# Causal attention on one core: four key tiles share one denominator matmul

## The reference

```python
x = x + _L0_attn_ref(_layernorm(x, axis=-1), wq, wk, wv, wo)     # causal attention, 32 query heads, 8 key heads of 32
x = x + _L0_ffn_ref(_layernorm(x, axis=-1), ...)                 # a mixing layer
x = x + _L1_attn_ref(_layernorm(x, axis=-1), Wq, Wk, Wv, Wo)     # causal attention again
x = x + _L1_ffn_ref(_layernorm(x, axis=-1), ...)                 # experts
```

```python
scores = einsum('bqhd,bkhd->bhqk', q, k) / sqrt(32)   # masked above the diagonal
attn = softmax(scores, axis=-1)
out = einsum('bhqk,bkhd->bqhd', attn, v)
```

## Time and profile before

| | us |
|---|---|
| time of the program, median of 3 executions | 3196.64 (3193.96 to 3196.96) |
| span of the profiled execution, first to last instruction | 3192.5 |
| TensorE matmul busy in the span | 2861.6 (90%) |
| VectorE busy | 2039.7 (64%) |
| ScalarE busy | 1004.8 (31%) |
| GpSimd busy | 282.5 (9%) |
| 3072 matmuls of the denominators, busy together | 329.9 |

### The profile page before, as it was taken

One profiled execution on the slowest core, in us unless ns is written; L12 is line 12 of the kernel. 1 busy time (PEld: TensorE's weight loads), 2 busy tenths in 40 slices (PEclk: granted clock), 3 DMA queues, 4 the chain that ended last, 5 costly groups with the idle time before them and its releaser, 6 DMA issues. The chain is left out here.

```text
span 3192.5 us, 48849 instructions
## 1 busy us (share of the span) xinstructions
PE 2861.6 (90%) x16848; PEld 1854.1 (58%) x16848; DVE 2039.7 (64%) x3303; ACT 1004.8 (31%) x1549; POOL 282.5 (9%) x397
## 2 busy tenths in 40 slices
PE   7999998999999799752869999989999997897999
PEld 6555454655554488642656555546555553786887
DVE  7676677767776433588776766767677774324443
ACT  2234334224334411252521433433234334201000
POOL 1011011001110000000010001011011110001111
PEclk9999999999999899875979999999999999998999
DMA  4322222323121322000133213213313120544111
GB/s 154 91 62 86 62 61 80 111 63 101 54 81 51 124 84 75 0 0 0 79 132 116 75 53 87 69 55 103 104 53 100 53 80 20 193 138 152 67 63 43
DMA packets 121063, 253.16 MB, mean 79 GB/s; under 512 B 12720, under 2 KB 39728, under 8 KB 120880
## 3 DMA queue, kind: packets, MB, share of 16 engines
q1 hardware_dynamic: 120912, 251.03, 24.8%
HBM read 166.57 MB, written 84.41 MB: 79 GB/s over the span
## 5 line engine op out<-in xcount | busy, mean ns | idle before, releaser
L597 DVE TENSOR_REDUCE a_mx<-a_psh 128x1 f32<-128x512 f32 (+3 forms) x1216 | 773.2, 660 | 351.5 <-PE a_psh L743 236.8
L502 ACT ACTIVATE a_prob<-a_pst 128x1024 f32<-128x1024 f32 (+3 forms) x768 | 595.9, 816 | 823.3 <-PE a_pst L789 821.0
L738 PE MATMUL a_psh<-a_kst,a_qst 96*128 96x512 f32 (+3 forms) x1536 | 543.6, 404 | 9.4 <-DVE a_mx L597 3.4
L738 PEld LDWEIGHTS a_psh<-a_kst,a_qst 96*128 96x128 f32 x1536 | 287.4, 192 | 396.8 <-DVE a_mx L597 327.4
L789 PE MATMUL a_pst<-a_qst,a_kst 97*128 97x512 f32 (+2 forms) x1536 | 424.3, 377 | 46.6 <-issue 17.5
L809 PE MATMUL a_ppv<-a_prob,a_vg 128*32 128x512 f32 (+3 forms) x3072 | 333.7, 507 | 12.5 <-POOL a_prob L436 11.1
L789 PEld LDWEIGHTS a_pst<-a_qst,a_kst 97*128 97x128 f32 x1536 | 256.6, 196 | 138.6 <-issue 72.3
L809 PE MATMUL a_pden<-a_prob,a_ones 128*32 128x512 f32 (+3 forms) x3072 | 329.9, 502 | 0.0
L436 POOL TENSOR_SCALAR_AFFINE_SELECT a_prob<-a_prob 128x512 f32<-128x512 f32 x256 | 178.6, 698 | 1383.7 <-ACT a_prob L502 1383.7
L641 DVE RECIPROCAL a_dens<-a_dens 128x512 f32<-128x512 f32 x64 | 214.6, 3353 | 68.2 <-ACT a_dens L510 55.2
L743 PE MATMUL a_psh<-a_negmask,a_identb 128*128 128x128 bf16 x1024 | 228.7, 232 | 0.0
(11 more groups left out here) (213 smaller groups left out, 3786.8 us busy)
## 6 DMA issues: line engine op xcount, KB each, us to landing
a_qst<-q SPq DMA_DIRECT2D x192, 256.0 KB, 4.5
a_wraw<-in_wqkv SPq DMA_DIRECT2D x52, 512.0 KB, 5.6
q<-a_stg_hi SPq DMA_DIRECT2D x64, 256.0 KB, 2.5
q<-a_stg_lo SPq DMA_DIRECT2D x64, 256.0 KB, 2.8
oT<-a_oT SPq DMA_DIRECT2D x64, 256.0 KB, 2.5
a_kst<-kT SPq DMA_DIRECT2D x96, 128.0 KB, 3.0
h_oraw<-oT SPq DMA_DIRECT2D x16, 512.0 KB, 4.1
h_x<-in_x SPq DMA_DIRECT2D x16, 512.0 KB, 4.7
```

Source lines behind the costliest of these rows:

```text
L502: act.activation(prob[k % 2][:, 2 * half:2 * half + 2, off:], pst[:, half, :, off:], ACT.Exp, scale=scale).then_inc(s["exp_done"], 1)
L597: dve.tensor_reduce(mx_hq[kc][:, heads[0]:heads[0] + m, qt], psh[:, at, 0:m * n].rearrange("p (m n) -> p m n", n=n), AX.X, ALU.max)\
L738: mm = pe.matmul(psh[:, at, i * n:(i + 1) * n], qst[par][0:96, h, qt * P:(qt + 1) * P], kst[par][0:96, kc * BANK:kc * BANK + n], start=Tru ...
```

## The change

Units 4 to 7 are called held. It holds for all orders but `ahead7`, so for 30 groups.

- ScalarE writes the exponentials of unit 4 into `acc`, which is `xin0` (heads 0, 1) and `xin1` (heads 2, 3), and not into `prob`.
- The four denominator steps den 4 to den 7 are gone. PV 4 reads `acc`.
- For units 5, 6 and 7 GpSimd adds the first half of `prob` to `acc[0]` and VectorE the second half to `acc[1]`, each one instruction of 128 x 1024 elements. GpSimd's comes where ST k.1 stands in the list, VectorE's where den k stood.
- At den 9, behind that unit's own 4 matmuls, 4 matmuls over `acc` bring the sum into the denominators. They wait for both chains of additions.
- ScalarE's exponentials of units 7, 8 and 9 wait, beside what they waited for, for GpSimd's addition of unit 5, 6 and 7 (first half) and VectorE's (second half), since these read the `prob` that is overwritten.
- SyncE waits in `ahead7` for the last PV of the group before, ahead of its first load into `xin0`.
- The `_turn` semaphores are counted up beside the waits and nobody waits for them.

```diff
@@ -45,6 +45,9 @@
 UNITS = [(qc, ki) for qc in range(NQC) for ki in range(4 * qc + 4)]
 NU = len(UNITS)
 DIAGONAL = [e for e, (qc, ki) in enumerate(UNITS) if ki >= 4 * qc]
+FIRST_FULL = UNITS.index((1, 0))
+ADDED = [e for e, (qc, ki) in enumerate(UNITS) if qc == 1 and 1 <= ki <= 3]
+SUMMED_AT = UNITS.index((1, 5))
 CHUNK_END = [e for e, (qc, ki) in enumerate(UNITS) if ki == 4 * qc + 3]
 
 
@@ -200,7 +203,7 @@
         "wl0", "wl1", "w_hi", "w_ready", "sh_ready", "sh_free", "roped", "q_hi", "q_lo", "v_ready",
         "k_out", "q_out", "qs00", "qs01", "qs10", "qs11", "ks0", "ks1", "mx_ready", "mT_ready", "m_out", "mr0", "mr1", "st_ready",
         "exp_done", "mask_done", "pv_done", "acc_copied", "norm_done", "vg_ready", "os0", "os1",
-        "pool_turn", "sp_turn", "pe_turn")}
+        "pool_added", "dve_added", "pool_turn", "act_turn", "dve_turn", "sp_turn", "pe_turn")}
     x_first, x_loaded = [s[f"xf{i}"] for i in range(NX_BUF)], [s[f"xl{i}"] for i in range(NX_AHEAD)]
     w_loaded = (s["wl0"], s["wl1"])
     max_row, o_stored = (s["mr0"], s["mr1"]), (s["os0"], s["os1"])
@@ -261,6 +264,7 @@
                                          for p in prob for i in range(2)]
 
 
+        acc = [x[:, :].rearrange("p (h n) -> p h n", n=BANK) for x in xin]
         x_next = [x[:, :] for x in xin] + [vT[:, :], wraw[0][:, :, :].rearrange("p k n -> p (k n)")]
         mx_hq = [mx[:, i, :].rearrange("p (h q) -> p h q", q=ST_) for i in range(2)]
         block = ctx.enter_context(nc.Block())
@@ -276,6 +280,12 @@
         def psh_banks(k, half):
 
             return psh[:, half, :]
+
+        def exps(order, e, half):
+
+            if order is not ahead7 and e == FIRST_FULL:
+                return acc[half]
+            return prob[e % 2][:, 2 * half:2 * half + 2, :]
 
         def batches(eng, batch):
 
@@ -363,6 +373,8 @@
 
                             sp.wait_ge(s["w_ready"], W0 + (b + 1) * N_WCHUNK + 1)
                             sp.sem_inc(s["sp_turn"], 1)
+                            sp.wait_ge(s["pv_done"], PV0 + n * NU)
+                            sp.sem_inc(s["sp_turn"], 1)
                         if k >= NX_AHEAD:
 
                             sp.wait_ge(s["zT_ready"], ZT0 + ((b + 1) * ST_ + k - NX_AHEAD) * 2 + 2)
@@ -436,6 +448,17 @@
                         pool.affine_select(out=blk, in_=blk, compare_op=ALU.is_ge, fill=0.0, base=0,
                                            pattern=[[0, GH], [1, P]], channel_multiplier=-1)\
                             .then_inc(s["mask_done"], 1)
+                    if what == "ST" and half == [1] and e in ADDED and order is not ahead7:
+
+                        pool.wait_ge(s["exp_done"], E0 + (n * NU + e) * 2 + 2)
+                        if e == ADDED[0]:
+                            pool.sem_inc(s["pool_turn"], 1)
+                            pool.wait_ge(s["pv_done"], PV0 + n * NU + FIRST_FULL + 1)
+                        else:
+                            pool.sem_inc(s["pool_turn"], 1)
+                            pool.wait_ge(s["pool_added"], (b * (NG - 1) + g) * len(ADDED) + ADDED.index(e))
+                        pool.sem_inc(s["pool_turn"], 1)
+                        pool.tensor_tensor(acc[0], acc[0], exps(order, e, 0), ALU.add).then_inc(s["pool_added"], 1)
                     if what == "XS":
                         reciprocal_deviation((b + 1) * ST_ + e, e)
                 if order is body:
@@ -498,8 +521,13 @@
                         if half == 0:
 
                             act.wait_ge(s["pv_done"], n * NU + k + 1)
+                        if k - 2 in ADDED and order is not ahead7:
+
+                            adds = (b * (NG - 1) + g) * len(ADDED) + ADDED.index(k - 2) + 1
+                            act.wait_ge((s["pool_added"], s["dve_added"])[half], adds)
+                            act.sem_inc(s["act_turn"], 1)
                         act.wait_ge(s["st_ready"], ST0 + (n * NU + k) * 2 + half + 1)
-                        act.activation(prob[k % 2][:, 2 * half:2 * half + 2, off:], pst[:, half, :, off:],
+                        act.activation(exps(order, k, half)[:, :, off:], pst[:, half, :, off:],
                                        ACT.Exp, scale=scale).then_inc(s["exp_done"], 1)
                     if what == "PV" and part == [1] and k in CHUNK_END:
                         q = n * 2 + CHUNK_END.index(k)
@@ -630,6 +658,16 @@
                         normalise((b + 1) * ST_ + k, x_next[k % NX_AHEAD], k)
                     if what == "XC":
                         xT_lo((b + 1) * ST_ + k, k, psh_banks)
+                    if what == "PV" and step[2] == 1 and k in ADDED and order is not ahead7:
+
+                        if k == ADDED[0]:
+                            dve.wait_ge(s["pv_done"], PV0 + n * NU + FIRST_FULL + 1)
+                        else:
+                            dve.wait_ge(s["dve_added"], (b * (NG - 1) + g) * len(ADDED) + ADDED.index(k))
+                        dve.sem_inc(s["dve_turn"], 1)
+                        dve.wait_ge(s["exp_done"], E0 + (n * NU + k) * 2 + 2)
+                        dve.sem_inc(s["dve_turn"], 1)
+                        dve.tensor_tensor(acc[1], acc[1], exps(order, k, 1), ALU.add).then_inc(s["dve_added"], 1)
                     if what == "LO":
                         part_lo(b * RB + 4 + (g + 2 - k) * 2 + k, k)
                     if what == "WS":
@@ -804,11 +842,28 @@
                             if ki == 0:
 
                                 pe.wait_ge(s["acc_copied"], (n * 2 + qc) * 2 + 2)
-                        acc, lhs = ((ppv, vg[par][:, ki, :]), (pden, ones[:, :]))[part]
-                        for h in range(GH):
-                            mm = pe.matmul(acc[h * HD:(h + 1) * HD, off:], lhs, prob[k % 2][:, h, off:],
-                                           start=(ki == 0), stop=(ki == 4 * qc + 3), skip_group_check=True)
-                        if part == 1:
+                        if part == 0:
+                            for h in range(GH):
+                                mm = pe.matmul(ppv[h * HD:(h + 1) * HD, off:], vg[par][:, ki, :],
+                                               exps(order, k, h // 2)[:, h % 2, off:],
+                                               start=(ki == 0), stop=(ki == 4 * qc + 3), skip_group_check=True)
+                        held = order is not ahead7 and k in (FIRST_FULL, *ADDED)
+                        first_den = (ki == 4 if order is not ahead7 and qc == 1 else ki == 0)
+                        if part == 1 and not held:
+                            for h in range(GH):
+                                mm = pe.matmul(pden[h * HD:(h + 1) * HD, off:], ones[:, :], prob[k % 2][:, h, off:],
+                                               start=first_den, stop=(ki == 4 * qc + 3), skip_group_check=True)
+                        if part == 1 and k == SUMMED_AT and order is not ahead7:
+
+                            adds = (b * (NG - 1) + g + 1) * len(ADDED)
+                            pe.wait_ge(s["pool_added"], adds)
+                            pe.sem_inc(s["pe_turn"], 1)
+                            pe.wait_ge(s["dve_added"], adds)
+                            pe.sem_inc(s["pe_turn"], 1)
+                            for h in range(GH):
+                                mm = pe.matmul(pden[h * HD:(h + 1) * HD, :], ones[:, :], acc[h // 2][:, h % 2, :],
+                                               start=False, stop=False, skip_group_check=True)
+                        if part == (0 if held else 1):
                             mm.then_inc(s["pv_done"], 1)
 
             pe.wait_ge(s["const"], 1)
```

## The result

The changed kernel takes 3381.59 us (median of four executions, 3341.5 to 3408.5) against 3196.66 (3193.96 to 3196.96) before. The kernel is slower, as forecast, but by 177 us where 73 were forecast, and outside the range given. The profiled execution took 3374.12 us, with a span of 3372.4; TensorE's mean granted clock was 0.891 in it, and 0.947 before.

What follows compares the result with a forecast made beforehand. TensorE was taken to lead, with VectorE close behind through two banks. Terms -0.4 + 1.15 + 0.7 + 0.25 + 1.0 = +2.7 us in 28 groups, +75.6 on 3196.6, gave 3272, rounded to 3270; range 3228 to 3308.

Steps and rivals of the forecast that it cites:

- the chain of each unit: PV, S steps, their maxima, VectorE's addition, one more maximum, then the S step needing that bank; +2.7 us per group.
- unit 4: Den step gone and no addition: S12 comes earlier, the stalled start goes, PV 5 about 0.4 us earlier; term -0.4.
- unit 5: VectorE's addition waits for GpSimd's, ends at PV 5 +4.1; S19 starts at +4.85, before 3.70; term +1.15 us.
- unit 6: VectorE's addition, behind GpSimd's, ends at PV 6 +4.35; S25 starts at +5.1, before 4.42; term +0.7 us.
- unit 7: No GpSimd addition beside VectorE's, which ends at +3.77; S30 starts at +4.4, before 4.15; term +0.25 us.
- the sum at unit 9: Four matmuls over `acc` at den 9, neither waiting nor hidden: +1.0 us per group.
- Three of the prediction's signs: `pden` busy time falls about 90 us; S matmuls wait 60 us or more for maxima; VectorE's unit 5 addition about 1.9 us.
- the later addition waits for the earlier: When VectorE's and GpSimd's additions meet, the later waits for the earlier's end; unit 5's ends at +2.9 + 1.2 = +4.1.
- The other reading, both slowed all along: Both engines slowed while additions overlap, VectorE to about 0.37 of its pace; sum 0.1 us smaller per group.
- rival 4: Additions collide more or TensorE's clock falls: a group loses 3.9 us or more, 3306 us and beyond; chance 0.14.
- `body7`: The two groups without S steps: TensorE's saving held back by GpSimd's additions; bounds -1 and +2 us per group, taken at 0.
- The cover named for GpSimd's additions: One 2.4 us addition per about 5 us unit costs nothing; without cover, unit 8's mask and PV 8 would be late.

Runs made afterwards that it cites:

- Experiment 2: Changed kernel with all additions and waits kept, but TensorE makes all denominators as before and the matmuls over the sum are left out: 3268.94 us, ratio 1.0234.
- experiment 1: Changed kernel without the additions on both engines and their waits, so the denominators lack units 5 to 7: 3131.57 us, ratio 0.9804.
- experiment 5: Changed kernel with VectorE's addition one place earlier in its queue, at PV k's first part, GpSimd not made to wait: 3163.34 us, ratio 0.9906.
- experiment 3: Changed kernel with GpSimd's additions for units 6 and 7 waiting until VectorE's for the unit before is done: 3283.02 us, ratio 1.0278.
- experiment 6c: Changed kernel with VectorE's addition one place earlier and S steps spread again by TensorE's real columns, GpSimd not made to wait: 3154.75 us, ratio 0.9882.

## Why the prediction was wrong

**Right: what bounds, and the chain of each unit.** VectorE's queue behind the two banks of S was the path. By the steps of the prediction, in the group that kept its clock: unit 4 -0.40 (said -0.4); unit 5 +1.37 (+1.15), with S19 at PV 5 + 5.08 (+4.85); unit 6 +0.75 (+0.7), with S25 at PV 6 + 5.07 (+5.1); unit 7 +0.17 (+0.25), its addition 1.22 alone; the sum at unit 9 +0.87 (+1.0). Together 2.76, forecast 2.7. Experiment 2 shows the same waits, and experiment 1 the same path without additions. The unit 5 difference is small and is where GpSimd started: 0.97 after PV 5 (516.90), not 0.5. Three of the prediction's signs came as well: the matmuls into `pden`, the sum's included, are busy 236.4 us where they were 329.9, 93.5 less (said 90), the S matmuls wait 102.9 us for maxima (said 60 or more), and VectorE's addition for unit 5 is stretched, to 2.30 (said 1.9).

**Right: the later addition waits for the earlier.** 2.30 where 1.22 is the time alone, an end 1.1 after GpSimd's, and in experiment 5 the reverse. The Trainium skill, "SBUF — State Buffer", section "Who interferes with whom", calls the shared pair of ports an exclusive lock and says that the order of issue decides who blocks; that it is held for the whole instruction it says where it speaks of VectorE's two-port modes. These rows agree with a lock for the whole instruction, in both directions. The other reading, both slowed all along, falls: the engine that began first was not slowed in the changed kernel (2.36). In experiment 5 VectorE's was not either (1.22).

**The step that failed: the clock, for which the sum has no term.** The prediction left "the clock falls" to rival 4, which shares its chance of 0.14 with a worse collision. The new idle ahead of S19 was foreseen, at about 1.5 us (it is 1.85), and was said to lie near the two stretches of the earlier trace rows, busy 1.90 of 3 us at a clock of 1.00 and 1.45 at 0.54. But the rest of the stretch was not added up. With den 5 gone there are only S17, S18 and half of ST 7 between S16 and S19, and TensorE's busy time is well below both:

```profile
397.40:400.40 3.00, 0.97 (x3) 0.49 (x3) 3.00 (x4) 1.02 (x1) 1.30 (x1) 0.97 0.00 0
```

The clock then fell in 26 of 28 groups and stayed down for 3 to 20 us, mostly 10 or 20, in which the matmuls take nearly twice as long: 122 us in all. The prediction's own sign for rival 4, a granted clock under 0.95 in the stage, came: 0.89 from the first group to the last of layer 0, before 0.98. Rival 4 had the right cause, but its price began at 1.2 us per group over the forecast (3306, "and beyond"); measured are 4.4. Experiments 2 and 5 show it by its absence: with more work on TensorE between the waits, or with the waits shortened, the mean clock is 0.942 and 0.948, and the time 105 and 211 us less than the changed kernel's.

**Mis-sized: `body7`.** Taken at 0 with bounds -1 and +2, measured +3.1 and +3.3. The cover named for GpSimd's additions was lost, by the path that the prediction named for it: the three run back to back, the mask of unit 8 is late behind them, and PV 8 waits.

```profile
1158.60 1.93 PE L847 MATMUL a_ppv<-a_prob,a_vg 128*32 128x512 f32 x8 [2.03 <-POOL a_prob L448]
```

```profile
1150.55 3.13 POOL L461 TENSOR_TENSOR a_xin<-a_xin,a_prob 128x1024 f32<-128x1024 f32 x1 [0.18 <-POOL a_xin L461]
```

The PV at 1158.60 again runs at the low clock (1.93). GpSimd's additions also take more here (3.13), beside VectorE's, which the estimate of 7.1 us left out; VectorE's take up to 3.2.

**Not seen: the four waits at group starts**, 29 us in the trace of before, which the shorter program lost. That hid part of the loss: had they stayed, the result would have been about 3403.

**Open.** In the group of the rows at 515.93 the same wait (1.82 us) with the same little work (0.97 of the 3 us from 518.00 on) left the clock at 1.00; in most groups it fell. What decides this was not tried. That the kernel's times spread over 67 us, where the kernel before spreads over 3, fits a clock that falls in some groups of one execution and not of another (the four executions had mean clocks of 0.891, 0.877, 0.886 and 0.906 for 3374, 3409, 3389 and 3342 us), but no single group was followed through two executions.

## What to carry to other kernels

When work is taken off the busiest engine and a wait takes its place, add up that engine's busy time over the whole stretch round the wait, and price the half-speed work behind it: here the chain of waits and the sum cost 77 us, and the clock that fell after the waits 122. When additions on two engines hold each other up, arrange that the engine that others wait for starts first, and put the added instruction where no bank is asked for right behind it; that one line was worth 211 us here. After such a change, let the planner count the work as it now stands, and look at the program's length too.

## What the runs showed that was not expected

- The fallen clock did not come back with the work: TensorE was busy 1.75 to 2.00 of each 2.00 us from 401 on, and its clock at 0.50 until about 410, in 16 other groups for 17 to 20 us. In the 28 groups it fell with no single wait longer than 1.85 us, in experiment 3 with none longer than 0.77 in the group shown. The Trainium skill, "TensorE: Matmul & The Clock Gate", section "A second HAM failure mode: psum-queue depth-cycling", tells of a kernel that cycles through PSUM banks, whose short idle times between groups of matmuls make the clock go down and up; the rows at 400.43 and 879.98 are short waits for PSUM banks with such a fall behind them, and agree.
- TensorE's first ST of a group stood 4.2 to 4.6 us with no releaser in the trace, four times in each of the three kernels with 109 or 110 packets (1.8 MB) on the instruction queue, and never in the nine with 71 (1.16 MB).
- GpSimd's addition of 128 x 1024 took 2.36 us alone and up to 3.48 beside VectorE's (experiment 6c).
